# Moving token normalisation and routing weights from VectorE to GpSimd in a transformer layer with attention and experts

## The chip, the cores and the metric

The kernel runs on one core of a Trainium2 chip. The metric is device time in microseconds, from start to end of one execution of the whole program. The core has a matrix engine (TensorE, PE in the profile, with its weight loads PEld), VectorE (DVE), ScalarE (ACT), GpSimd (POOL) and SyncE (SP, which here only issues DMAs). Each engine works through its own instructions in their order, and they wait for one another through semaphores.

## The reference

A batch of 8 sequences of 512 tokens, 128 wide, goes through one pre-normalised layer. All is float32.

```
x = x + attention(layernorm(x))      # 16 heads of 64, relative-position bias, softmax
x = x + experts(layernorm(x))        # 16 experts, each token takes its best 4

logits = -dist2(x, keys) + x @ rw.T + rb
topv, topi = top_k(logits, 4)
w = softmax(topv)
expert(x) = gelu(x @ w1.T + b1) @ w2.T + b2
out = sum(w[k] * expert[topi[k]](x) for k in range(4))
```

## The kernel before

**Attention.** The eight sequences are the batches b = 0 to 7 (`LAST` is 7). A batch has 8 steps i = 0 to 7, one for each pair of heads, and a step has four visits v = 0 to 3, one for each block of 128 queries, with two heads hh in each. So there are 64 steps in a row, all written out. What a step does for its visits is spread over engines: TensorE makes the scores (L1288), VectorE adds the bias and finds the maximum (`scores`, L1020, semaphore `neg_rdy`), ScalarE takes the exponential (L863), VectorE the reciprocal of the sum (L1026, `rinv_rdy`), and GpSimd multiplies the probabilities by it (`normalise_probs`, L795, two instructions of 128x512 a visit, `norm_rdy`). Visits 0 and 1 are then transposed by VectorE (`turn_blocks`, L1036) and by a round trip through DRAM (tile `turned` out to `pt_dram`, back as `pt_d`); visits 2 and 3 by TensorE in the next step (`weights_t`, L1302). TensorE multiplies both by the values (L1314 for the late half, L1325 for the early half, which waits for `pt_d`). In the middle of a step it also projects queries, keys and values for the next step (L1239 to L1241).

**What TensorE waits for in a step.** Visit 3's scores need the first maximum of this step. The second transpose of visit 3 of the step before (L1302, hh = 1) needs the fifth maximum, which VectorE makes as visit 2's first. L1314 needs the seventh maximum, which stands behind VectorE's transposes of visit 0, and these wait for GpSimd's `norm_rdy` of visit 0.

**Routing** of batch b-1 is laid between the steps of batch b by small tables (`ROUTE_DVE`, `ROUTE_POOL`, ...), which give for a step the stages that each engine does there. GpSimd computes the reciprocal deviation (`rstd`, L342) at step 2, visit 2; VectorE normalises the tokens into `copies` (stage 3, L383, in `early_extras`) in step 3; TensorE transposes them (L315) and makes the logits (L320) at the end of step 3; VectorE finds the best four, their slots (L445, L448) and, at the end of step 5, the routing weights (stages 10 to 12, L424, L427, L430). GpSimd scatters the tokens to `xs_dram` with 16 indirect DMAs (L363) from step 5 on; the first of them waits for the slots. In step 6 VectorE normalises the next batch's tokens into `xn` (L383, shown as tile `xt`, which shares its memory), and TensorE transposes them at the step's end (L1233).

**Experts.** After attention, 79 blocks of 256 token rows go through their expert, eight of them in each turn of a loop, some turns written out. TensorE turns a block's rows (L1391), makes the hidden layer (L1403 to L1405) and the second product (L1416); GpSimd scatters the result with two indirect DMAs a block (`block_out`, L830). The last batch's routing is spread over the first blocks by tables named `TAIL_...`. SyncE loads the rows of block 32 only after all token scatters have landed (`rest`). At the end VectorE adds the weighted results to the tokens (`combine`).

Of the kernel before, what the change touches and what calls it, by code (L numbers as in the profile page):

```python
# [29 lines left out]
P = 128  # L30
# [7 lines left out]
def layer_kernel(nc, x, wq, wk, wv, wo, rel_bias, onehot, ident, expert_no, before_tok, region, home_row, pad,  # L38
# [47 lines left out]
    with ExitStack() as ctx:  # L86
# [248 lines left out]
        def route_pool(pool, n, stage_no):  # L335
            if stage_no == "rstd":
# [5 lines left out]
                pool.tensor_tensor(rstd[:, 1], var_eps[:, 1], minus_half[:], ALU.pow).then_inc(rstd2, 1)  # L342
            elif stage_no == "copy":
# [36 lines left out]
        def normalise(dve, n, q, to, ready, done):  # L380
            dve.wait_ge(ready, n + 1)
            for c in range(TC):
                dve.tensor_scalar(to[:, c, :], x_all[:, bass.ds(n * TC + c, 1), :], moments[:, q, c, 0:1],  # L383
                                  rstd[:, q, c:c + 1], ALU.subtract, ALU.mult).then_inc(done, 1)

        def route_dve(dve, n, stage_no):
# [5 lines left out]
            elif stage_no == 3:  # L392
                normalise(dve, n, 1, copies[:, :, 0, 0:D], rstd2, xn2)
# [34 lines left out]
            elif stage_no == 12:  # L428
                dve.wait_ge(ei_rdy, n + 1)
                dve.tensor_tensor(wt[:, bass.ds(n * TC, TC), :], ev[:], einv[:].unsqueeze(2).broadcast_to([P, TC, TOP]),  # L430
                                  ALU.mult).then_inc(wt_rdy, 1)
# [107 lines left out]
        ROUTE_DVE_LATE = {3: (4, 5, 6), 4: (13, 14), 5: (10, 11, 12)}  # L539
# [3 lines left out]
        ROUTE_POOL = {(2, 2): ("rstd",), (3, 2): ("copy",)}  # L543
# [61 lines left out]
        TAIL_DVE = {5: (3,), 7: (4, 5, 6), 8: (7, 8, 9), 9: (10, 11, 13, 14), 10: (12, 15, 16)}  # L605
        TAIL_POOL = {1: ("rstd",), 3: ("copy",)}
        TAIL_POOL.update({8 + q: (2 * q, 2 * q + 1) for q in range(6)})
        TAIL_POOL.update({14 + q: (12 + q,) for q in range(4)})
# [4 lines left out]
        def complete(n):  # L613

            return min(NBLK, max(EARLY + NE, (S * TOP * (n + 1) + NE * (BLK - 1)) // BLK))
        assert max(TAIL_POOL) < PEEL
# [160 lines left out]
        def _(pool):  # L777
# [20 lines left out]
            def step(b, i):  # L798
                for v in range(TC):
# [4 lines left out]
                    if (i, v) == ((4, 1) if b == 0 else (0, 3)) and b < LAST:  # L804
                        rsqrt(b + 1)
                    for n, q in scatters_at(b, i, v):
                        route_pool(pool, n, q)
# [182 lines left out]
        def _(dve):  # L990
# [73 lines left out]
            def early_extras(b, i):  # L1064

                if i == NPR - 2 and b < LAST:
                    normalise(dve, b + 1, 0, xn, rstd_rdy, xn_rdy)
                if i == 3 and exists(b - 1):
                    route_dve(dve, b - 1, 3)

# [38 lines left out]
            def combine(n, k):  # L1109

                dve.wait_ge(ld_y[n % YB][k], 16 * (n // YB + 1))
# [491 lines left out]
```

## Time and profile before

| | |
|---|---|
| time before, median of 3 (lowest to highest) | 1126.33 us (1124.82 to 1127.68) |
| profiled execution: time, span of instructions | 1125.26 us, 1123.4 us |
| busy: TensorE, VectorE, ScalarE, GpSimd | 94%, 77%, 75%, 61% of the span |
| granted TensorE clock, mean | 0.989 of full speed |
| chain that ended last, by engine | PE 75%, DVE 11%, DMA 5%, issue 4%, POOL 4% |

The busy shares say which engine could bound a stage, and the chain says which did. In brackets behind an instruction of a timeline stands how long its engine sat idle before it, and whose end released it. A matmul's end is modelled, and matmuls overlap, so step lengths are better taken from the start of one step's first score matmul to that of the next.

### The profile page before, as it was taken

Reading aid. Unit: us, or ns where it says so; the run is one execution under the profiler, and the core shown is the slowest. Engines: PE = TensorE matmul, PEld = TensorE weight load, DVE = VectorE, ACT = ScalarE, POOL = GpSimd, SP = SyncE. Lnnn points to the kernel's source line nnn. Section 1 sums busy time; section 2 is a strip of 40 time slices with the busy share of each in tenths; the row PEclk is TensorE's granted clock in tenths of the full one; section 3 lists DMA queues with packets and bytes.
Section 4 is the critical chain, followed back from the end, with each engine's and each line's share of the span. In section 5 each row is a group of like instructions: output and inputs, shape, how many; then the busy total and the mean of one; then the engine's idle time right before and its main releaser. Section 6 shows DMA issues by size and latency. Waiting matters only on the chain.

```text
span 1123.4 us, 27427 instructions
## 1 busy us (share of the span) xinstructions
PE 1059.4 (94%) x8477; PEld 863.0 (77%) x8478; DVE 862.0 (77%) x2576; ACT 842.5 (75%) x2050; POOL 684.0 (61%) x882
## 2 busy tenths in 40 slices
PE   8999998999999999999999999999889999999993
PEld 4777776777677777767776776777679999999993
DVE  6788789888888888888988889798726544457775
ACT  5788777877787788778877877787757677766661
POOL 4654545774676477467656755764746777655553
PEclk9999999999999999999999999999989999999997
DMA  7776776665666567567656765687852733224552
GB/s 209 215 213 187 209 218 195 185 186 165 182 188 180 163 192 191 154 180 201 182 154 186 204 167 165 186 258 229 253 168 77 164 87 89 78 77 149 158 173 66
DMA packets 138223, 193.27 MB, mean 172 GB/s; under 512 B 19320, under 2 KB 110976, under 8 KB 138096
## 3 DMA queue, kind: packets, MB, share of 16 engines
q1 hardware_dynamic: 128944, 174.84, 55.6%
q0 software_dynamic: 9152, 16.88, 4.5%
q8 instruction: 62, 1.02, 0.4%
q14 instruction: 65, 0.53, 0.2%
HBM read 103.27 MB, written 90.33 MB: 172 GB/s over the span
## 4 chain that ended last, share of the span: by engine, by line
PE 75%; DVE 11%; DMA 5%; issue 4%; POOL 4%; SPq 1%; ACT 1%; DVEq 0%; POOLq 0%; ACTq 0%
PE bank L1416 12%; PE bank L1288 12%; PE bank L1325 9%; PE bank L1314 9%; PE bank L1302 6%; DVE shared L1020 5%; PE bank L1403 3%; PE bank L1405 3%; PE bank L1404 3%; PE bank L1239 3%; PE bank L1241 3%; PE bank L1240 3%; PE bank L1336 3%; POOL shared L795 3%; DMA pt_d<-pt_dram 2%
## 5 line engine op out<-in xcount | busy, mean ns | idle before, releaser
L795 POOL TENSOR_SCALAR shared<-shared,rinv 128x512 f32<-128x512 f32 x512 | 352.4, 700 | 262.5 <-DVE rinv L1026 260.2
L863 ACT ACTIVATE shared<-shared,nmax 128x512 f32<-128x512 f32 x512 | 367.5, 728 | 85.7 <-DVE nmax L1020 84.5
L1020 DVE CUSTOM_DVE_ANT_0 shared<-bank,shared 128x512 f32<-128x512 f32 x512 | 329.0, 680 | 78.9 <-PE bank L1302 26.9
L830 POOL DMA_INDIRECT y_dram<-yb,home x158 | 160.7, 1017 | 93.4 <-issue 49.0
L1036 DVE STREAM_TRANSPOSE turned<-shared 128x512 f32<-128x512 f32 x256 | 166.3, 687 | 14.1 <-issue 14.1
L363 POOL DMA_INDIRECT xs_dram<-copies,slot x128 | 135.1, 1056 | 61.5 <-issue 47.7
L869 ACT ACTIVATE pt_e<-bank 128x512 f32<-128x512 f32 x256 | 146.6, 595 | 31.1 <-PE bank L1302 30.4
L1302 PE MATMUL bank<-idn,shared 128*128 128x128 f32 x1024 | 139.7, 277 | 18.7 <-DVE nmax L1020 18.6
L1416 PE MATMUL bank<-shared,act_h 128*128 x1264 | 154.1, 275 | 1.2 <-DVE yb L1141 0.7
L1416 PEld LDWEIGHTS bank<-shared,act_h 128*128 128x128 f32 x1264 | 148.0, 192 | 1.8 <-issue 1.8
L1302 PEld LDWEIGHTS bank<-idn,shared 128*128 128x128 f32 x1024 | 112.8, 141 | 45.2 <-issue 29.1
L1314 PE MATMUL bank<-pt_e,v_sb 128*64 128x256 f32 x1024 | 124.6, 385 | 5.2 <-DVE nmax L1020 4.6
L895 ACT ACTIVATE act_h<-bank,shared 128x256 f32<-128x256 f32 x316 | 124.2, 476 | 3.4 <-PE bank L1405 3.2
L1325 PE MATMUL bank<-pt_d,v_sb 128*64 128x256 f32 x1024 | 122.7, 381 | 2.7 <-DMA pt_d<-pt_dram 2.7
L1288 PE MATMUL bank<-k_hi,q_lo 64*128 64x512 f32 x512 | 109.6, 422 | 12.5 <-DVE nmax L1020 9.4
L1314 PEld LDWEIGHTS bank<-pt_e,v_sb 128*64 128x64 f32 x1024 | 69.2, 136 | 52.5 <-issue 23.2
L863 ACT ACTIVATION_READ_ACCUMULATOR shared<-shared,nmax 128x1 f32 x512 | 104.5, 204 | 0.0
L1325 PEld LDWEIGHTS bank<-pt_d,v_sb 128*64 128x64 f32 x1024 | 73.8, 137 | 36.5 <-issue 4.7
L1288 PE MATMUL bank<-k_hi,q_hi 64*128 64x512 f32 x512 | 101.6, 390 | 0.0
L1288 PE MATMUL bank<-k_lo,q_hi 64*128 64x512 f32 x512 | 101.5, 390 | 0.0
L1403 PE MATMUL bank<-xbt_hi,w_lo 128*128 128x256 f32 x316 | 96.2, 305 | 4.1 <-DVE w_lo L1129 4.1
L1141 DVE TENSOR_TENSOR yb<-bank,shared 128x256 f32<-128x256 f32 x79 | 33.5, 425 | 78.7 <-PE bank L1416 78.4
(154 smaller groups left out, 1904.0 us busy)
## 6 DMA issues: line engine op xcount, KB each, us to landing
pt_dram<-turned SPq DMA_DIRECT2D x512, 128.0 KB
pt_d<-pt_dram SPq DMA_DIRECT2D x128, 512.0 KB, 4.4
xb<-xs_dram SPq DMA_DIRECT2D x79, 129.0 KB
shared<-in_experts SPq DMA_DIRECT2D x16, 514.0 KB, 5.3
shared<-y_dram SPq DMA_DIRECT2D x32, 256.0 KB, 5.0
shared<-roll_dram SPq DMA_DIRECT2D x4, 768.0 KB, 8.2
y_dram<-yb,home POOLq DMA_INDIRECT x158
xs_dram<-pad_sb SPq DMA_DIRECT2D x17, 129.0 KB, 2.3
```

The costliest lines, as they stand in the source:

```text
L363: pool.indirect_dma_start(xs_dram, bass.IndirectOffsetOnAxis(ap=slot[:, c * TOP + k:c * TOP + k + 1], axis=0), copies[:, c, k % 2, :], Non ...
L795: pool.tensor_scalar(tile, tile, rinv[:, 2 * v + hh:2 * v + hh + 1], 1.0, ALU.mult, ALU.mult)\
L830: pool.indirect_dma_start(y_dram, bass.IndirectOffsetOnAxis(ap=home[:, j, c:c + 1], axis=0), yb[:, j, c, :], None, bounds_check=last_row, ...
L863: act.activation(prob[:, v, hh, :], prob[:, v, hh, :], ACT.Exp, bias=nmax[:, n:n + 1], scale=-1.0, accum_out=rsum[:, n:n + 1]).then_inc(ex ...
L869: act.activation(pt_e[:, hh, :, (v - 2) * P:(v - 1) * P], weights_bank(b, i, v, hh)[:].rearrange("p (j q) -> p j q", j=TC), ACT.Copy)\
L1020: dve.tensor_tensor_reduce(prob[:, v, hh, :], score_bank(v, hh)[:], strips[:, 2 * i + hh, v * P:v * P + S], -1.0, BIG, ALU.add, ALU.min, n ...
L1036: dve.transpose(turned[:, v, :, :, hh, :].rearrange("p k j r -> p j k r"), prob[:, v, hh, :].rearrange("p (j k c) -> p j k c", k=TC, c=BK) ...
L1288: mm = pe.matmul(score_bank(v, hh)[:], q[rows, i % 2, v * P:(v + 1) * P], k[rows, i % 2, :], start=(m == 0), stop=(m == 2))
L1302: mm = pe.transpose(weights_bank(b, i, v, hh)[:, j * P:(j + 1) * P], prob[:, v, hh, j * P:(j + 1) * P], idn[:])
L1314: pe.matmul(ps_a[DH * hh:DH * hh + DH, 2 * P:4 * P], v_sb[:, i // 2 % 2, j, col:col + DH], pt_e[:, hh, j, :], start=(j == 0), stop=(j == T ...
L1325: mm = pe.matmul(ps_a[DH * hh:DH * hh + DH, 0:2 * P], v_sb[:, i // 2 % 2, j, col:col + DH], pt_d[:, :, :, j, hh, :].rearrange("p v a r -> ...
L1416: mm = pe.matmul(ps_y[:, c * D:(c + 1) * D], act_h[:, q % 2, f, c * P:(c + 1) * P], params[:, bass.ds(w + (W2 + f * D), D)], start=(f == 0 ...
```

## The change

Three pieces of elementwise work go from VectorE's program to GpSimd's: the routing normalisation (to step 2, visit 2, right behind `rstd`), the next batch's normalisation (from step 6 to step 4, visit 3), and the product that makes the routing weights (from the end of step 5 to step 6, visit 1, behind the scatter there). The two instructions before that product stay on VectorE. `combine` waits for the weights through a semaphore, as another engine now makes them. For the last batch, GpSimd issues one token scatter behind each of the blocks 8 to 23, where it issued two behind each of the blocks 8 to 13 and one behind each of the blocks 14 to 17.

```diff
             elif stage_no == "rstd":
...
                 pool.tensor_tensor(rstd[:, 1], var_eps[:, 1], minus_half[:], ALU.pow).then_inc(rstd2, 1)
+                normalise(pool, n, 1, copies[:, :, 0, 0:D], rstd2, xn2)
+            elif stage_no == "weights":
+                pool.wait_ge(ei_rdy, n + 1)
+                pool.tensor_tensor(wt[:, n * TC:(n + 1) * TC, :], ev[:], einv[:].unsqueeze(2).broadcast_to([P, TC, TOP]),
+                                   ALU.mult).then_inc(wt_rdy, 1)
...
-        def normalise(dve, n, q, to, ready, done):
-            dve.wait_ge(ready, n + 1)
+        def normalise(eng, n, q, to, ready, done):
+
+            eng.wait_ge(ready, n + 1)
             for c in range(TC):
-                dve.tensor_scalar(to[:, c, :], x_all[:, bass.ds(n * TC + c, 1), :], moments[:, q, c, 0:1],
+                eng.tensor_scalar(to[:, c, :], x_all[:, n * TC + c, :], moments[:, q, c, 0:1],
                                   rstd[:, q, c:c + 1], ALU.subtract, ALU.mult).then_inc(done, 1)
...
-        ROUTE_DVE_LATE = {3: (4, 5, 6), 4: (13, 14), 5: (10, 11, 12)}
+        ROUTE_DVE_LATE = {3: (4, 5, 6), 4: (13, 14), 5: (10, 11)}
...
-        ROUTE_POOL = {(2, 2): ("rstd",), (3, 2): ("copy",)}
+        ROUTE_POOL = {(2, 2): ("rstd",), (3, 2): ("copy",), (6, 1): ("weights",)}
...
-        TAIL_DVE = {5: (3,), 7: (4, 5, 6), 8: (7, 8, 9), 9: (10, 11, 13, 14), 10: (12, 15, 16)}
+        TAIL_DVE = {7: (4, 5, 6), 8: (7, 8, 9), 9: (10, 11, 13, 14), 10: (15, 16)}
...
-        TAIL_POOL.update({8 + q: (2 * q, 2 * q + 1) for q in range(6)})
-        TAIL_POOL.update({14 + q: (12 + q,) for q in range(4)})
+        TAIL_POOL.update({8 + q: (q,) for q in range(SCATTERS)})
...
+        TAIL_POOL[10] = ("weights",) + TAIL_POOL[10]
...
+                    if (i, v) == (4, 3) and b < LAST:
+                        if exists(b - 1):
+                            pool.wait_ge(l_rdy, b)
+                        else:
+                            pool.wait_ge(xhi_rdy, b + 1)
+                        normalise(pool, b + 1, 0, xn, rstd_rdy, xn_rdy)
...
-            def early_extras(b, i):
-
-                if i == NPR - 2 and b < LAST:
-                    normalise(dve, b + 1, 0, xn, rstd_rdy, xn_rdy)
-                if i == 3 and exists(b - 1):
-                    route_dve(dve, b - 1, 3)
-
...
                 dve.wait_ge(ld_y[n % YB][k], 16 * (n // YB + 1))
+                dve.wait_ge(wt_rdy, n + 1)
...
-                early_extras(b, i)
```

GpSimd's program in batch 1, from step 1's last probabilities to the copies of step 3, before (L342 is the routing's `rstd`, L348 and L349 are the stage "copy"):

```order
L795 TENSOR_SCALAR shared<-shared,rinv 128x512 x14
L342 TENSOR_TENSOR rstd<-var_eps,minus_half 128x4
L795 TENSOR_SCALAR shared<-shared,rinv 128x512 x8
L348 COPY copies<-copies 128x4x128
L349 COPY copies<-home_sb 128x8
L795 TENSOR_SCALAR shared<-shared,rinv 128x512 x12
L363 DMA xs_dram<-copies,slot 69888x129
```

Here two visits' worth of probabilities follow `rstd` directly. The same place now, where L389 is the line in `normalise`, L353, L354 and L368 are the former L348, L349 and L363:

```order
L342 TENSOR_TENSOR rstd<-var_eps,minus_half 128x4
L389 TENSOR_SCALAR copies<-x_all,moments,rstd 128x128 x4
L795 TENSOR_SCALAR shared<-shared,rinv 128x512 x8
L353 COPY copies<-copies 128x4x128
L354 COPY copies<-home_sb 128x8
L795 TENSOR_SCALAR shared<-shared,rinv 128x512 x10
L389 TENSOR_SCALAR xt<-x_all,moments,rstd 128x128 x4
L795 TENSOR_SCALAR shared<-shared,rinv 128x512 x2
L368 DMA xs_dram<-copies,slot 69888x129
```

Four instructions stand in front of visit 3's probabilities of step 2, and four in front of visit 0's of step 5; no other instruction of GpSimd's changed places here.

VectorE's program in batch 1, from the slots of step 5 to the second maximum of step 6's visit 0, and on to its visit 2, before (the ISA rows are the maximum, L1020, and the read of its result):

```order
L1036 STREAM_TRANSPOSE turned<-shared 128x4x4x32 x2
L1026 RECIPROCAL rinv<-rsum 128x2
L424 TENSOR_REDUCE esum<-ev 128x4
L427 RECIPROCAL einv<-esum 128x4
L430 TENSOR_TENSOR wt<-ev,einv 128x16
L1026 RECIPROCAL rinv<-rsum 128x2
L1020 ISA shared,nmax<-bank,shared 128x512
...
L1026 RECIPROCAL rinv<-rsum 128x2
L383 TENSOR_SCALAR xt<-x_all,moments,rstd 128x128 x4
L1020 ISA shared,nmax<-bank,shared 128x512
```

Step 6's first maximum stands behind the product, and visit 2's behind the normalisation. Now (L1042, L1032, L1026 are the former L1036, L1026, L1020):

```order
L1042 STREAM_TRANSPOSE turned<-shared 128x4x4x32 x2
L1032 RECIPROCAL rinv<-rsum 128x2
L428 TENSOR_REDUCE esum<-ev 128x4
L431 RECIPROCAL einv<-esum 128x4
L1032 RECIPROCAL rinv<-rsum 128x2
L1026 ISA shared,nmax<-bank,shared 128x512
...
L1032 RECIPROCAL rinv<-rsum 128x2
L1026 ISA shared,nmax<-bank,shared 128x512
```

The product `wt` is gone from before step 6's maxima and the four normalisations from the middle of them; in step 3 the four L383 into `copies` are gone from the same place.

## Rows read from the trace of the kernel before

**Rows 1.** Who waited for whom: us in total, times, longest; TensorE's waits for VectorE.

```profile
PE bank L1302 <- DVE nmax L1020: 18.6, 15, 2.1
PE bank L1288 <- DVE nmax L1020: 9.4, 7, 1.7
```

**Rows 2.** Stretch, its length, busy time by engine: batch 5's step 2.

```profile
537.73:549.25 11.52, 11.52 (x94) 8.78 (x92) 9.80 (x34) 9.84 (x24) 8.50 (x11) 1.00 0.77 208
```

**Rows 3.** The same view, sums of six steps: step 3, then step 6, batches 1-6.

```profile
sum 88.71, PE 80.34 PEld 60.73 DVE 78.57 ACT 63.30 POOL 51.04; mean PE 13.39 PEld 10.12 DVE 13.09 ACT 10.55 POOL 8.51
sum 90.50, PE 75.27 PEld 55.08 DVE 86.35 ACT 63.37 POOL 58.00; mean PE 12.54 PEld 9.18 DVE 14.39 ACT 10.56 POOL 9.67
```

**Rows 4.** Timeline of TensorE in batch 5's steps 3 and 6: start, us.

```profile
554.03 0.60 PE L1302 MATMUL bank<-idn,shared 128*128 128x128 f32 x4
556.03 0.63 PE L1302 MATMUL bank<-idn,shared 128*128 128x128 f32 x4 [1.40 <-DVE nmax L1020]
561.17 1.06 PE L320 MATMUL bank<-rk,xt 128*128 128x16 f32 x8
591.38 0.50 PE L1288 MATMUL bank<-k_hi,q_lo 64*128 64x512 f32 x2 [1.40 <-DVE nmax L1020]
595.85 0.63 PE L1302 MATMUL bank<-idn,shared 128*128 128x128 f32 x4 [1.16 <-DVE nmax L1020]
598.60 0.60 PE L1233 MATMUL bank<-idn,xt 128*128 128x128 f32 x4
```

**Rows 5.** Timeline of VectorE in the same two steps: the three pieces that move.

```profile
552.87 2.40 DVE L383 TENSOR_SCALAR copies<-x_all,moments,rstd 128x128 f32<-128x128 f32 x4
589.11 1.55 DVE L430 TENSOR_TENSOR wt<-ev,einv 128x16 f32<-128x16 f32 x1
593.16 1.94 DVE L383 TENSOR_SCALAR xt<-x_all,moments,rstd 128x128 f32<-128x128 f32 x4
```

**Rows 6.** GpSimd by group: mean ns of one stands behind the busy time.

```profile
L795 POOL TENSOR_SCALAR shared<-shared,rinv 128x512 f32<-128x512 f32 x512 | 352.4, 700 | 262.5 <-DVE rinv L1026 260.2
L830 POOL DMA_INDIRECT y_dram<-yb,home x158 | 160.7, 1017 | 93.4 <-issue 49.0 <-DVE yb L1141 36.4 <-DVE home L1139 7.9
L342 POOL TENSOR_TENSOR rstd<-var_eps,minus_half 128x4 f32<-128x4 f32 x8 | 8.4, 1049 | 1.2 <-issue 1.2
L348 POOL COPY copies<-copies 128x512 f32<-128x512 f32 x8 | 4.9, 616 | 0.0
L349 POOL COPY copies<-home_sb 128x8 f32<-128x8 f32 x8 | 1.5, 193 | 0.0
```

**Rows 7.** Timeline of GpSimd, batch 5's steps 3 to 5.

```profile
552.25 2.69 POOL L795 TENSOR_SCALAR shared<-shared,rinv 128x512 f32<-128x512 f32 x4
576.52 2.99 POOL L795 TENSOR_SCALAR shared<-shared,rinv 128x512 f32<-128x512 f32 x4 [3.52 <-DVE rinv L1026]
585.48 1.11 POOL L363 DMA_INDIRECT xs_dram<-copies,slot  x1 [4.12 <-issue]
```

**Rows 8.** Timeline, batch 5's step 5: VectorE's transposes of visit 0, TensorE's L1314.

```profile
581.57 1.30 DVE L1036 STREAM_TRANSPOSE turned<-shared 128x512 f32<-128x512 f32 x2
584.04 1.95 PE L1314 MATMUL bank<-pt_e,v_sb 128*64 128x256 f32 x16
```

**Rows 9.** Timeline, batch 5's step 6: reads of the DRAM round trip, and their use.

```profile
590.63 2.38 SPq L675 DMA_DIRECT2D pt_d<-pt_dram  x2
600.91 1.90 PE L1325 MATMUL bank<-pt_d,v_sb 128*64 128x256 f32 x16
```

**Rows 10.** The page, DMA issues: KB each, median us from issue to landing.

```profile
pt_d<-pt_dram SPq DMA_DIRECT2D x128, 512.0 KB, 4.4
```

**Rows 11.** Timeline of GpSimd, batch 7's step 3.

```profile
753.88 1.04 POOL L342 TENSOR_TENSOR rstd<-var_eps,minus_half 128x4 f32<-128x4 f32 x1 [1.18 <-issue]
```

**Rows 12.** Timeline among the experts: GpSimd's last token scatter, TensorE's turn of block 32.

```profile
915.11 0.96 POOL L363 DMA_INDIRECT xs_dram<-copies,slot  x1 [0.30 <-issue]
939.12 0.38 PE L1391 MATMUL bank<-idn,xb 128*128 128x128 f32 x2
```

More of the change, by code:

```diff
@@ L391, in route_dve @@
                 moments_of(dve, n, 1, stage_no, st2, mv2, ve2)
-            elif stage_no == 3:
-                normalise(dve, n, 1, copies[:, :, 0, 0:D], rstd2, xn2)
             elif stage_no == 4:
@@ L427, in route_dve @@
                 dve.reciprocal(einv[:], esum[:]).then_inc(ei_rdy, 1)
[L428 to L431, printed above, removed]
             elif stage_no == 13:
```

## Prediction

> **What bounds the kernel now.** TensorE is busy for nearly all of the span, so I look for the time in which it is not, and for who ends it. The list of waits names two large entries, both for VectorE's maxima: 18.6 us in front of L1302 and 9.4 us in front of L1288, 28.0 us together [rows 1]. The lengths of the steps say where they lie. A step in which nothing is added takes 11.52 us, all of it TensorE's [rows 2]. Over batches 1 to 6, step 3 takes 88.71 / 6 = 14.79 us and step 6 takes 90.50 / 6 = 15.08 us [rows 3], and VectorE is busy for 13.1 and 14.4 us of these. The timeline of TensorE shows one wait in step 3, 1.40 us before the second half of visit 3's transposes, and two in step 6, 1.40 us before visit 3's scores and 1.16 us before the same transposes [rows 4]. All three end with a maximum. In front of those maxima VectorE does just the three pieces that the change moves: 2.40 us of normalisation in step 3, the product of 1.55 us ahead of step 6, and 1.94 us of normalisation in it [rows 5]. So each lies on the path that sets the end, but only as far as TensorE waits.
>
> **What can be had.** Step 6 needs, beside the 11.52 us, the four token transposes; they take 0.53 us, from 598.60 to the next work (four L1302 of the same size are 0.60 long [rows 4]). Its floor is 12.05 us, and 15.08 - 12.05 = 3.03 us can go, of which 2.56 us are the two waits and the rest is TensorE's slow start after each. The two removals are 1.55 and 1.94 us, 3.49 us together, more than the 3.03 us, and no VectorE work replaces them. Six batches give 18.2 us. Batch 0 has only the normalisation, and I give it what that costs in batch 5, some 1.1 us. In batch 7 only the product is removed, and the step has expert loads beside it; I give nothing for it (at most 1.4 us, its wait's size elsewhere).
>
> Step 3 needs 11.52 us, the transposes of the copies (0.53 us as above) and the logits (1.06 us [rows 4]), 13.1 us, with some 0.1 us between them. So 14.79 - 13.2 = 1.6 us can go, but here the work comes back on GpSimd's queue in front of what TensorE needs.
>
> **What one instruction costs on GpSimd.** No row shows a 128x128 normalisation there. Below it is bounded by the copy of 8 elements a partition, 0.19 us, above by the same kind of instruction on 512 elements, 0.70 us, and further off by L342, which takes 1.05 us for 4 elements [rows 6]. Copies say how the cost grows: (616 - 193) / 504 = 0.84 ns per element. The same start-up of 0.19 us and 0.98 ns per element for L795 make 0.19 + 128 x 0.98 = 0.31 us. The subtraction and product are two operations as L795's are, so I take its line and not L342's power. Four one behind another are 1.2 us, and about 0.15 us is added for waiting on `rstd` of its own engine, 1.35 us. The product of 16 elements is near 0.2 us and stands at step 6, visit 1, where nobody waits for it.
>
> The Trainium skill (GPSIMD Engine Reference, Engine selection) speaks against the move: elementwise work belongs on VectorE, as GpSimd takes about twice as long where there are two inputs. With one input tensor it calls the two engines about equal. VectorE's normalisations in step 6 are 1.94 / 4 = 0.49 us each; equal would make the sum some 1106 us, twice as long would end near rival 4. No run here shows either on GpSimd yet.
>
> **Step 3 with GpSimd's four.** They stand between `rstd`, which ends at 552.25, and step 2's last probabilities, 2.69 us for two pairs there [rows 7], so 1.35 us for a pair. TensorE's L1302 halves would without waiting start at 554.03 and 554.56, and they need the two halves of this pair. Their second is ready at 552.25 + 1.35 + 1.35 + 0.05 = 555.0 us. The wait is 0.45 us, and with a restart of 0.15 us and some rounding 0.65 us of the 1.6 us stay. VectorE's transposes of visit 0 wait behind the next pair, until 555.6 and 556.3; the seventh maximum then comes at about 557.5, and TensorE asks for it at about 558.3. Gain: 0.95 us in six batches, 5.7 us. In batch 7, `rstd` itself waits for the scatters before it and ends at 754.92 [rows 11], 1.2 us later in the step than in batch 5, so the wait is 0.45 + 1.2 = 1.65 us, where it is now the longest of its kind, 2.1 us [rows 1]: 0.5 us.
>
> **Step 4 and 5.** The next batch's four stand behind step 4's last pair, which ends at 579.51 [rows 7], and in front of step 5's visit 0. That pair would be done at 580.86 + 1.36 = 582.2, its first half at 581.5; VectorE wants the first at 581.57 and the second 0.65 us later [rows 8]. It fits with nothing left over. TensorE's L1314 at 584.04 leaves another 0.6 us, so the stall here is zero up to about 2.0 us for the four and grows one to one beyond. After this GpSimd idles 4.12 us before the first scatter, which waits for slots [rows 7], and the lateness ends there. Nothing else of its queue is late: with the product gone, VectorE's first maximum comes at 589.8 and TensorE asks at 590.0.
>
> **The round trip through DRAM** is the next limit in step 6. Its second read is issued near 592.7 and lands some 4.4 us later, near 597.2 [rows 9, 10]. TensorE takes it at 600.91, and with 3.03 us gone at 597.9. The read does not start earlier, since GpSimd's slots set it. So 0.7 us are left and I charge nothing.
>
> **Tail.** Matrix work bounds it, and the VectorE work taken out there lies beside it. The token scatters now end behind block 23, not 17. At 916.07 GpSimd is through with them [rows 12] and with the results of 18 blocks; it now has 12 result scatters more ahead of its last token scatter, each 1.02 us [rows 6] and 0.3 us of issue, so that one starts no later than 931.7. With 4 us allowed for it to land (the reads of [rows 10] take 4.4) and 2.2 us to load a block (half of what four times the bytes take [rows 10]), block 32's rows are there by 938, and TensorE turns them at 939.12 [rows 12]. I charge nothing; a microsecond or two more would show one to one.
>
> **Sum.** 18.2 + 1.1 + 5.7 + 0.5 = 25.5 us off the profiled 1125.26 us is 1099.8. That execution is 1.1 us below the median of 1126.33, against which the forecast is 1100.8; I say 1101.
>
> **Rivals.**
> 1. *GpSimd's instructions cost by the piece*, 0.70 us as on 512 elements [rows 6]. Four and the wait are 2.95 us. Step 3 waits 2.05 + 0.2 us where 1.6 us were to go: 0.65 us worse. Step 5 stalls 1.1 us. A batch gains 3.03 - 0.65 - 1.1 = 1.3 us; six give 8, batch 0 nothing, batch 7 waits 3.25 us where it now waits 2.1, 1 us worse: 1119 us. For it: the start-up of this kind of instruction is unseen. Against: copies scale with their elements. 7 in 100.
> 2. *The round trip takes part back.* If the read lands 1 to 1.5 us later (or the write before it does), TensorE waits that much in six batches: 6 to 9 us back, 1107 to 1110. For it: only 0.7 us are left. 12 in 100.
> 3. *No wait on GpSimd at all*: its four take 0.8 us or less (0.2 us each, near the small copies). Then step 3 gives its whole 1.6 us: 1096 to 1097. 15 in 100.
> 4. *The other side: GpSimd becomes the bound.* If an instruction costs what L342 does, 1.05 us, four are 4.35 us. Step 3 then waits 3.65 us for 1.6 us removed, step 5 2.5 us: 2.05 + 2.5 - 3.03 = 1.5 us worse a batch, 9 us in six; batch 0 adds 2.5 - 1.1 = 1.4 and batch 7 2.5, 13 us in all: 1139 us. It decides from about 0.9 us per instruction. Against: L342 is a power. 3 in 100.
> 5. *Nothing moves*, since another engine ends the same waits, ScalarE for one: against it, it idles in both steps (10.55 us busy of 14.8 [rows 3]). 2 in 100.
>
> The forecast has the other 61. The range takes rivals 2 and 3 and most of what lies between: 1095 to 1110. A measurement here tells 0.3%, 3.4 us, from no change: faster 0.93, same 0.04, slower 0.03.
>
> **What would show it.** In the changed profile, step 6 near 12.1 us and step 3 near 13.8; L389 near 0.3 us on GpSimd; no wait before L1302 for a maximum, but some 0.5 us before its second half in step 3, behind GpSimd's probabilities; VectorE idle before its transposes of visit 0 in step 3. The forecast is wrong if L389 takes over 0.5 us, or if L1325 waits for `pt_d` in step 6.

## The result, and the profile after

The change makes the kernel slower: 1131.89 us (median of 13 runs, 1128.18 to 1136.33) against 1126.33 us (13 runs, 1124.07 to 1130.25). The ratio is 1.0048, with a 95% interval of 1.0031 to 1.0064. The profiled execution took 1130.02 us with a span of 1128.2 us, 4.8 us more than the span of before, and its mean granted TensorE clock is 0.984 where it was 0.989.

The page's busy times, and the list of waits, TensorE's alone (us in total, times, longest):

```profile
PE 1061.5 (94%) x8477; PEld 870.4 (77%) x8478; DVE 822.8 (73%) x2508; ACT 841.2 (75%) x2050; POOL 733.8 (65%) x950
```

```profile
PE bank L1301 <- POOL shared L795: 14.7, 7, 2.6
PE bank L1313 <- DVE nmax L1026: 14.0, 14, 1.7
PE bank L1324 <- DMA pt_d<-pt_dram: 6.8, 8, 2.6
...
PE bank L1287 <- DVE nmax L1026: 1.7, 6, 0.5
...
PE bank L1301 <- DVE nmax L1026: 0.6, 1, 0.6
```

L1301 and L1287 are the former L1302 and L1288. Their waits for VectorE, 28.0 us in [rows 1], are gone but for 2.3 us. In their place stand 14.7 us in which the same transposes wait for GpSimd's probabilities, and 14.0 us in front of L1313 (the former L1314). The first seven are the step 3 of each batch with routing; of the 14.0 us, 7.9 (six times 1.31 to 1.33) stand in step 5 of batches 1 to 6.

Now the sums of batches 1 to 6 (the view of [rows 3]) for step 3, step 5 and step 6. The fourth line is step 5 of before:

```profile
sum 97.54, PE 85.45 PEld 64.94 DVE 66.37 ACT 64.23 POOL 69.25; mean PE 14.24 PEld 10.82 DVE 11.06 ACT 10.71 POOL 11.54
sum 77.38, PE 69.46 PEld 56.08 DVE 54.78 ACT 59.68 POOL 54.60; mean PE 11.58 PEld 9.35 DVE 9.13 ACT 9.95 POOL 9.10
sum 77.05, PE 74.43 PEld 55.73 DVE 67.27 ACT 62.01 POOL 58.60; mean PE 12.41 PEld 9.29 DVE 11.21 ACT 10.33 POOL 9.77
```

```profile
sum 69.04, PE 69.04 PEld 53.25 DVE 55.80 ACT 59.72 POOL 38.74; mean PE 11.51 PEld 8.88 DVE 9.30 ACT 9.95 POOL 6.46
```

Step 6 gives 90.50 - 77.05 = 13.5 us back, as meant. Step 3 takes 97.54 - 88.71 = 8.8 us more and step 5 77.38 - 69.04 = 8.3 us more. Batch 0's step 6 is 1.2 us shorter and its step 5 0.8 us longer. What is left of the 4.8 us, some 1.5 us, is mostly made of two parts that no term names: the first score matmul of the program starts 2.4 us earlier (14.62 us where it was 17.05), and batch 0's step 1 takes 3.5 us more, with a wait of 2.61 us for `pt_d` (0.69 us before) and two falls of the granted clock to 0.50, 3.41 us each, where there was one before. What makes that wait longer isn't shown.

What one moved instruction costs, by its line in `normalise` (ns min/median/max), and the product on its new line:

```profile
L389 POOL TENSOR_SCALAR copies<-x_all,moments,rstd x32: 777/782/1065, 151.8 to 851.6; 128x128 f32<-128x128 f32 x32
L389 DVE TENSOR_SCALAR xt<-x_all,moments,rstd x4: 341/344/418, 7.4 to 8.2; 128x128 f32<-128x128 f32 x4
```

```profile
L346 POOL TENSOR_TENSOR wt<-ev,einv x8: 220/224/237, 200.2 to 883.5; 128x16 f32<-128x16 f32 x8
```

A normalisation takes 0.78 us on GpSimd, where the forecast had 0.31. The timeline of batch 5, first GpSimd's around step 3's start, then TensorE's in the same step:

```profile
554.51 1.04 POOL L342 TENSOR_TENSOR rstd<-var_eps,minus_half 128x4 f32<-128x4 f32 x1
555.67 3.12 POOL L389 TENSOR_SCALAR copies<-x_all,moments,rstd 128x128 f32<-128x128 f32 x4
558.78 2.68 POOL L795 TENSOR_SCALAR shared<-shared,rinv 128x512 f32<-128x512 f32 x4
```

```profile
552.57 0.50 PE L1287 MATMUL bank<-k_hi,q_lo 64*128 64x512 f32 x2
...
556.46 1.06 PE L1335 MATMUL bank<-wo_sb,ctxt 128*128 128x128 f32 x8
559.51 1.60 PE L1301 MATMUL bank<-idn,shared 128*128 128x128 f32 x8 [2.00 <-POOL shared L795]
...
569.61 0.50 PE L1287 MATMUL bank<-k_hi,q_lo 64*128 64x512 f32 x2
```

The four end at 558.78; the first of the pair behind them takes 0.67 us, and at about 559.5 TensorE can go on, after 2.00 us. The same in step 5, GpSimd, VectorE and TensorE:

```profile
585.07 3.12 POOL L389 TENSOR_SCALAR xt<-x_all,moments,rstd 128x128 f32<-128x128 f32 x4
588.17 1.36 POOL L795 TENSOR_SCALAR shared<-shared,rinv 128x512 f32<-128x512 f32 x2
```

```profile
588.95 1.33 DVE L1042 STREAM_TRANSPOSE turned<-shared 128x512 f32<-128x512 f32 x2 [1.70 <-issue]
```

```profile
591.01 1.30 PE L1313 MATMUL bank<-pt_e,v_sb 128*64 128x256 f32 x10 [1.32 <-DVE nmax L1026]
```

The profile names no engine for VectorE's wait ("issue"), but the times fit: the first probabilities of GpSimd's pair are done at 588.17 + 0.68 = 588.85, and the transposes start at 588.95. So GpSimd's lateness goes through these transposes, which idle 1.70 us, to the seventh maximum behind them and so to TensorE.

Step 3 has a second loss. Its stretches in batch 5, cut at the wait and at the changes of the clock (length, busy time of PE, PEld, DVE, ACT, POOL, granted clock, DMA share, GB/s):

```profile
552.57:557.40 4.83, 4.83 (x42) 3.97 (x40) 3.70 (x13) 3.30 (x8) 4.11 (x6) 1.00 0.72 187
557.40:559.50 2.10, 0.11 (x1) 0.00 (x0) 0.70 (x4) 1.30 (x5) 2.10 (x4) 1.00 0.73 236
559.50:560.40 0.90, 0.88 (x6) 0.64 (x7) 0.00 (x0) 0.19 (x1) 0.90 (x2) 1.00 0.43 173
560.40:563.80 3.40, 3.40 (x14) 3.11 (x13) 2.59 (x7) 2.37 (x6) 1.82 (x4) 0.50 0.21 53
563.80:569.61 5.81, 5.81 (x47) 3.78 (x45) 4.10 (x20) 3.69 (x9) 2.65 (x5) 1.00 0.48 122
```

After the wait TensorE works at full clock for 0.9 us, and then the granted clock is 0.50, that is 1.2 GHz where it was 2.4, for 3.40 us. It falls so in three of the seven steps 3 with routing in this execution. Of batches 1 to 6, the three without a fall take 15.44 to 15.50 us, the three with one 16.80, 17.26 and 17.04: 4.6 us more together. Some 0.3 us of that is batch 4's own, whose step 3 takes 15.83 us in a_busy, where the clock holds; 4.3 us are left for the clock.

### The profile page after: what moved, and what is told of

It is laid out like the page before. It is cut to its first block and busy times, and to the rows that moved or that the text cites. A ratio compares the mean times of both kernels' runs of the same rounds, so it can differ in the third digit from the quotient of the medians.

```text
span 1128.2 us, 27442 instructions
## 1 busy us (share of the span) xinstructions
PE 1061.5 (94%) x8477; PEld 870.4 (77%) x8478; DVE 822.8 (73%) x2508; ACT 841.2 (75%) x2050; POOL 733.8 (65%) x950
## 5 line engine op out<-in xcount | busy, mean ns | idle before, releaser
L795 POOL TENSOR_SCALAR shared<-shared,rinv 128x512 f32<-128x512 f32 x512 | 350.3, 695 | 229.9 <-DVE rinv L1032 227.0
L1026 DVE CUSTOM_DVE_ANT_0 shared<-bank,shared 128x512 f32<-128x512 f32 x512 | 329.6, 681 | 86.7 <-issue 36.5
L836 POOL DMA_INDIRECT y_dram<-yb,home x158 | 163.8, 1037 | 87.0 <-issue 47.8
L1042 DVE STREAM_TRANSPOSE turned<-shared 128x512 f32<-128x512 f32 x256 | 166.7, 689 | 49.3 <-issue 48.8
L368 POOL DMA_INDIRECT xs_dram<-copies,slot x128 | 134.7, 1053 | 56.9 <-issue 44.0
L1301 PE MATMUL bank<-idn,shared 128*128 128x128 f32 x1024 | 139.5, 278 | 15.3 <-POOL shared L795 14.7
L1301 PEld LDWEIGHTS bank<-idn,shared 128*128 128x128 f32 x1024 | 113.1, 141 | 41.3 <-POOL shared L795 25.7
L1313 PE MATMUL bank<-pt_e,v_sb 128*64 128x256 f32 x1024 | 124.6, 385 | 14.6 <-DVE nmax L1026 14.0
L1324 PE MATMUL bank<-pt_d,v_sb 128*64 128x256 f32 x1024 | 124.7, 385 | 6.8 <-DMA pt_d<-pt_dram 6.8
L1313 PEld LDWEIGHTS bank<-pt_e,v_sb 128*64 128x64 f32 x1024 | 70.9, 136 | 60.7 <-issue 33.0
L1287 PE MATMUL bank<-k_hi,q_lo 64*128 64x512 f32 x512 | 109.5, 422 | 4.7 <-DVE k_lo L1004 2.4
L1324 PEld LDWEIGHTS bank<-pt_d,v_sb 128*64 128x64 f32 x1024 | 76.7, 138 | 40.5 <-issue 12.6
L1287 PE MATMUL bank<-k_lo,q_hi 64*128 64x512 f32 x512 | 101.8, 391 | 0.0
L1287 PE MATMUL bank<-k_hi,q_hi 64*128 64x512 f32 x512 | 101.5, 390 | 0.0
```

Source lines behind the costliest of these rows:

```text
L368: pool.indirect_dma_start(xs_dram, bass.IndirectOffsetOnAxis(ap=slot[:, c * TOP + k:c * TOP + k + 1], axis=0), copies[:, c, k % 2, :], Non ...
L795: pool.tensor_scalar(tile, tile, rinv[:, 2 * v + hh:2 * v + hh + 1], 1.0, ALU.mult, ALU.mult)\
L836: pool.indirect_dma_start(y_dram, bass.IndirectOffsetOnAxis(ap=home[:, j, c:c + 1], axis=0), yb[:, j, c, :], None, bounds_check=last_row, ...
L1026: dve.tensor_tensor_reduce(prob[:, v, hh, :], score_bank(v, hh)[:], strips[:, 2 * i + hh, v * P:v * P + S], -1.0, BIG, ALU.add, ALU.min, n ...
L1042: dve.transpose(turned[:, v, :, :, hh, :].rearrange("p k j r -> p j k r"), prob[:, v, hh, :].rearrange("p (j k c) -> p j k c", k=TC, c=BK) ...
L1287: mm = pe.matmul(score_bank(v, hh)[:], q[rows, i % 2, v * P:(v + 1) * P], k[rows, i % 2, :], start=(m == 0), stop=(m == 2))
```

## The experiments

The first four kernels ran on a chip on which the kernel before took 1163.43 us (11 runs; in the three parts traced there, the time from the first expert block to the end is 34 to 40 us longer than in the kernel before, and attention steps that a part doesn't touch are alike), the later ones where it took 1125.47 (17 runs) and 1125.20 (24 runs). Each ratio is to the kernel before on the same chip.

### m1_forms: what GpSimd's forms cost by themselves

A kernel of its own. It leaves out the whole computation and copies the input to the output; then GpSimd alone runs eight instructions of each form, with nothing beside it, and after it VectorE and then ScalarE do the normalisation.

```
pool.tensor_scalar(out, src(n), mean or 0.25 or none, rstd or 1.5 or 1.0, subtract or mult, mult)
```

> This kernel only copies the input to the output and leaves the whole layer out; beside that, GpSimd alone runs tensor_scalar in twelve forms, eight instructions each, one engine at a time. In the changed kernel one L389 (128 elements, subtraction and product, both operands read from a tile) took 0.78 us, where one L795 (512 elements, two products, one operand read from a tile and one constant) took 0.70. Theory A: the second operand read from a tile is dear: the form with one tile operand and a constant takes 0.3 us at 128 elements (0.19 + 128 x 0.98 ns), whatever the operations, and the form with two 0.78 us. Theory B: the subtraction is dear: every form with it takes 0.78 us, also with constants, and two products 0.3 us also with two tile operands. Theory C: a tensor_scalar costs some 0.7 us by the piece: all forms take 0.6 to 0.8 us at 16, 128, 256 and 512 elements. Theory D: GpSimd is held up in the kernel by VectorE, and all forms take 0.3 us at 128 elements here, where it is alone.

The groups by line. In the output's name s is a subtraction, m a product, p an operand from a tile and i a constant (sm_pp is the change's own form, mm_pi that of L795); m_p is a single product, s_tt a subtraction of two tensors, and the last line is sm_pp on VectorE, run after GpSimd was done:

```profile
L59 POOL TENSOR_SCALAR sm_pp<-x_all,mean,rstd 128x512 f32<-128x512 f32 x8 | 16.5, 2072 | 0.0
L66 POOL TENSOR_SCALAR sm_pp<-x_all,mean,rstd 128x256 f32<-128x256 f32 x8 | 9.6, 1218 | 0.0
L67 POOL TENSOR_TENSOR s_tt<-x_all,mean 128x512 f32<-128x512 f32 x8 | 8.0, 1038 | 0.0
L58 POOL TENSOR_SCALAR sm_pp<-x_all,mean,rstd 128x128 f32<-128x128 f32 x8 | 6.2, 791 | 0.0
...
L61 POOL TENSOR_SCALAR sm_pi<-x_all,mean 128x128 f32<-128x128 f32 x8 | 5.6, 715 | 0.0
L57 POOL TENSOR_SCALAR mm_pi<-x_all,rstd 128x512 f32<-128x512 f32 x8 | 5.4, 692 | 0.0
L63 POOL TENSOR_SCALAR sm_ii<-x_all 128x128 f32<-128x128 f32 x8 | 4.9, 642 | 0.0
L64 POOL TENSOR_SCALAR m_p<-x_all,rstd 128x128 f32<-128x128 f32 x8 | 4.7, 602 | 0.0
L60 POOL TENSOR_SCALAR mm_pp<-x_all,mean,rstd 128x128 f32<-128x128 f32 x8 | 3.4, 447 | 0.0
L65 POOL TENSOR_SCALAR sm_pp<-x_all,mean,rstd 128x16 f32<-128x16 f32 x8 | 3.3, 427 | 0.0
L56 POOL TENSOR_SCALAR mm_pi<-x_all,rstd 128x128 f32<-128x128 f32 x8 | 2.8, 371 | 18.6 <-DMA out<-x_all 18.6
...
L74 DVE TENSOR_SCALAR dve<-x_all,mean,rstd 128x128 f32<-128x128 f32 x8 | 2.1, 342 | 95.1 <-POOL s_tt L67 95.1
```

The pair of operations decides. Two products cost (692 - 371) / 384 = 0.84 ns an element; subtract and multiply cost (2072 - 427) / 496 = 3.3 ns. With constants alone the subtracting form still takes 642 ns against 371 (one tile operand), so it is not the operands: each further tile operand adds about 0.075 us (371 to 447, 642 to 715 to 791). A lone product, 602 ns, is slow as well, so "subtraction is slow" is too narrow; of the forms tried here only two products were quick. And 791 ns alone against 782 in the kernel leaves nothing to contention.

### p_weights, p_routing, p_next: one part of the change each

Each is the kernel before with one piece moved as the change moves it (the tables of the last batch's routing go with it and are left out here).

```diff
 p_weights:
...
-        ROUTE_DVE_LATE = {3: (4, 5, 6), 4: (13, 14), 5: (10, 11, 12)}
+        ROUTE_DVE_LATE = {3: (4, 5, 6), 4: (13, 14), 5: (10, 11)}
...
-        ROUTE_POOL = {(2, 2): ("rstd",), (3, 2): ("copy",)}
+        ROUTE_POOL = {(2, 2): ("rstd",), (3, 2): ("copy",), (6, 1): ("weights",)}
...
 p_routing:
                 pool.tensor_tensor(rstd[:, 1], var_eps[:, 1], minus_half[:], ALU.pow).then_inc(rstd2, 1)
+                normalise(pool, n, 1, copies[:, :, 0, 0:D], rstd2, xn2)
...
-                if i == 3 and exists(b - 1):
-                    route_dve(dve, b - 1, 3)
 p_next:
+                    if (i, v) == (4, 3) and b < LAST:
...
+                        normalise(pool, b + 1, 0, xn, rstd_rdy, xn_rdy)
...
-                if i == NPR - 2 and b < LAST:
-                    normalise(dve, b + 1, 0, xn, rstd_rdy, xn_rdy)
```

> The kernel before with only the routing weights' product moved to GpSimd. Theory 1 (the price of L389 on GpSimd explains the loss, the rest of the prediction holds): this part has no L389, so it shows the gain alone: step 6's first wait of 1.40 us and its restart go in batches 1 to 6, step 6 near 13.5 in place of 15.1 us, 9 to 10 us faster, 1117. Rival (VectorE's time was not what mattered in step 6, or other waits take its place): within 3 us of before.

> The kernel before with only the routing normalisation moved to GpSimd. Theory 1: its four instructions take 3.1 us in front of step 2's last probabilities; step 3 takes 15.5 in place of 14.8 us, 0.7 us in six batches and 0.4 in batch 7, about 4.6 us slower, and more where the granted clock falls below full in step 3 as it did in three of seven in the changed kernel (1.5 us each): 1130 to 1135. Rival (the loss comes from the next batch's normalisation or from the tail): within 2 us of before.

> The kernel before with only the next batch's normalisation moved to GpSimd, to step 4, visit 3. Theory 1: step 5 is 1.4 us longer (12.9 in place of 11.5) in seven batches, and step 6 loses its second wait and restart, 1.3 us or so; the first wait, behind the product, stays. Sum within 2 us of before. Rival (VectorE's 1.9 us in step 6 was all bound, and step 5's stall comes from the product or the slots): 8 us or more faster.

**p_weights** is faster: 1155.39 us, ratio 0.9927 (0.9908 to 0.9945). Step 6 of batches 1 to 6, in the view of sums, is 81.89 us where [rows 3] have 90.50:

```profile
sum 81.89, PE 74.23 PEld 55.13 DVE 77.99 ACT 63.30 POOL 58.68; mean PE 12.37 PEld 9.19 DVE 13.00 ACT 10.55 POOL 9.78
```

That is 1.43 us a batch, 8.6 us in six, and the kernel gains 8.0. This piece alone does nearly what it should (9 to 10 us were expected).

**p_routing** is slower: 1180.51 us, 1.0133 (1.0113 to 1.0153), more than the 1.004 to 1.008 expected of it. Its wait is the changed kernel's 2.00 us, but here all seven steps 3 with routing lose the clock: by the expectation's own prices, 4.6 us for the wait and 1.5 us for each of seven falls make 15.1 us, of the 17.1 measured. Batch 3's step 3, and the sum of six:

```profile
353.66:370.70 17.04, 15.03 (x106) 11.55 (x105) 11.09 (x43) 10.87 (x25) 11.58 (x17) 0.90 0.54 148
...
sum 101.98, PE 90.00 PEld 68.97 DVE 66.49 ACT 65.20 POOL 69.48; mean PE 15.00 PEld 11.50 DVE 11.08 ACT 10.87 POOL 11.58
```

**p_next** is slower too: 1171.69 us, 1.0065 (1.0048 to 1.0082), where no more than 2 us either way was expected. Step 5 takes 12.92 us a batch, as in the changed kernel. Step 6, freed of 1.94 us of VectorE's work, takes 92.33 / 6 = 15.39 us, more than before. The wait behind the normalisation is gone, but the one before visit 3's scores is 1.82 us where it was 1.40 [rows 4], and the mean clock of five of the six steps is 0.89; the first is the one without a fall, though its wait is 2.09 us. It takes 14.30 us where it took 15.36 before, so this piece alone gives back about 1.1 us in step 6 where the clock holds, and loses 1.4 in step 5. The longer wait comes down the queue from GpSimd: in batch 3 VectorE's transposes of step 5's visit 1 idle 1.55 us until the probabilities behind the first scatter are there, and the product and the first maximum stand behind them. TensorE's timeline in batches 1 and 3, then steps 6 of the same two:

```profile
192.07 0.50 PE L1293 MATMUL bank<-k_hi,q_lo 64*128 64x512 f32 x2 [2.09 <-DVE nmax L1026]
...
394.58 0.50 PE L1293 MATMUL bank<-k_hi,q_lo 64*128 64x512 f32 x2 [1.82 <-DVE nmax L1026]
```

```profile
187.65:201.95 14.30, 12.21 (x99) 9.17 (x98) 12.65 (x34) 10.33 (x25) 9.65 (x13) 1.00 0.60 166
...
390.42:406.01 15.59, 13.77 (x98) 10.51 (x96) 12.77 (x34) 10.44 (x25) 9.76 (x14) 0.89 0.53 151
```

The three parts add up to 0.9927 - 1 + 0.0133 + 0.0065 = +1.25%, where the whole is +0.48%: the product and the next batch's normalisation help each other in step 6 (together 13.5 us off in six batches, where the one alone gives 8.6 and the other alone, with its falls, takes 1.8 more), and the clock falls seven times in p_routing's step 3 and five times in p_next's step 6, but three times in the whole change. A part's price read alone was no price in the whole.

### a_cheap: the changed kernel with the cheap form

`normalise` multiplies by `rstd` and by 1.0, as L795 does. It leaves out the subtraction of the mean, so its values aren't those of the reference.

```diff
-                eng.tensor_scalar(to[:, c, :], x_all[:, n * TC + c, :], moments[:, q, c, 0:1],
-                                  rstd[:, q, c:c + 1], ALU.subtract, ALU.mult).then_inc(done, 1)
+                eng.tensor_scalar(to[:, c, :], x_all[:, n * TC + c, :], rstd[:, q, c:c + 1],
+                                  1.0, ALU.mult, ALU.mult).then_inc(done, 1)
```

> The changed kernel with the normalisations in the form whose price is low, one operand from a tile and the constant 1.0, two products: it multiplies by the reciprocal deviation and leaves out the subtraction of the mean (on VectorE for the first batch too). Theory 1 (the prediction's path was right, and only the price of one instruction was wrong): at 0.37 us each, four and the wait are 1.6 us in place of 3.25; step 3 waits 0.7 us on GpSimd and takes 14.0, step 5 takes 11.5 and step 6 12.1 to 12.6 us, no fall of the clock in step 3: 2.0 to 2.3% faster than before (ratio 0.977 to 0.981). Rival (GpSimd's queue costs something of its own in those places, or the round trip through DRAM takes the gain back): 1% faster or less.

1103.90 us, ratio 0.9795 (0.9776 to 0.9814). This one number turns the sign. By its line, the instruction takes:

```profile
L389 POOL TENSOR_SCALAR copies<-x_all,rstd x32: 361/371/651, 150.1 to 827.3; 128x128 f32<-128x128 f32 x32
```

Sums for step 3 (13.82 us each) and step 6 (12.59):

```profile
sum 82.94, PE 80.95 PEld 60.82 DVE 66.37 ACT 62.50 POOL 58.82; mean PE 13.49 PEld 10.14 DVE 11.06 ACT 10.42 POOL 9.80
...
sum 75.55, PE 73.58 PEld 55.78 DVE 65.01 ACT 62.01 POOL 55.69; mean PE 12.26 PEld 9.30 DVE 10.83 ACT 10.34 POOL 9.28
```

Step 5 is 11.53 us but for one batch of 13.61. No step 3 of batches 1 to 6 loses the clock; batch 7's does, behind a wait of 2.61 us. The waits of TensorE for `pt_d` are 8.4 us in all in this kernel, 2.7 before: some of them stand in step 6 (1.07 us in batch 5), which keeps 0.5 us above 12.05.

### a_next50: the changed kernel, the next batch's four one visit later

```diff
-                    if (i, v) == (4, 3) and b < LAST:
+                    if (i, v) == (5, 0) and b < LAST:
```

> The changed kernel with the next batch's normalisation one visit later, behind visit 0's probabilities of step 5 and ahead of the scatter there, where GpSimd sat idle for 4.1 us until the slots came. Theory 1: step 5 is 11.5 us again in place of 12.9 in seven batches, 9.6 us less than the changed kernel, and nothing else moves: 0.3 to 0.5% faster than before on a chip where step 3 loses its clock in some batches, same as before where in all. Rival (what step 5 loses is VectorE's or the slots'): time as the changed kernel.

1119.75 us, 0.9955 (0.9935 to 0.9976): faster than before. Behind visit 0 of step 5 the four lie in the 4.12 us in which GpSimd idles [rows 7]. Step 5 is back at 11.52 us a batch, and step 6 is at 73.72 / 6 = 12.29, so 0.55 us of the changed kernel's 12.84 go with the stall before it. Step 3 is as in the changed kernel, 97.43 us, with three falls. The step's sum:

```profile
sum 69.10, PE 69.10 PEld 53.44 DVE 55.83 ACT 59.73 POOL 57.24; mean PE 11.52 PEld 8.91 DVE 9.31 ACT 9.95 POOL 9.54
```

### a_spread and a_spread_tt: the same work where nobody waits, in two forms

Both put `rstd` a visit earlier, two normalisations in its old place and two behind step 3's visit 0, and the next batch's four behind step 5's visit 0. a_spread_tt also writes each pair as a subtraction and a product of two tensors.

```diff
-        ROUTE_POOL = {(2, 2): ("rstd",), (3, 2): ("copy",), (6, 1): ("weights",)}
+        ROUTE_POOL = {(2, 1): ("rstd",), (2, 2): ("first half",), (3, 0): ("second half",), (3, 2): ("copy",), (6, 1): ("weights",)}
...
-                    if (i, v) == (4, 3) and b < LAST:
+                    if (i, v) == (5, 0) and b < LAST:
...
 a_spread_tt, in normalise:
+            eng.tensor_tensor(to[:, cs, :], x_all[:, n * TC + part[0]:n * TC + part[1], :],
+                              moments[:, q, cs, 0:1].broadcast_to(shape), ALU.subtract).then_inc(centred, 1)
...
+            eng.tensor_tensor(to[:, cs, :], to[:, cs, :], rstd[:, q, cs].unsqueeze(2).broadcast_to(shape), ALU.mult).then_inc(done, h)
```

> The changed kernel with the same instructions in other places of GpSimd's queue: the reciprocal deviation one visit earlier (step 2, visit 1), two of the routing's four normalisations at step 2, visit 2 and two behind visit 0's probabilities of step 3, and the next batch's four at step 5, visit 0. Theory 1: in front of step 2's last probabilities stand 1.6 us in place of 4.2 us, near the 1.05 us of before, so step 3 waits 0.5 us or less, takes 13.3 to 13.8 us and keeps its clock; step 5 11.5, step 6 12.1 to 12.6: 2.0 to 2.5% faster than before. Rival (the transposes of visit 0 in step 3 wait for GpSimd instead, and L1313 after them): step 3 at 14.5 or more, 1.5% faster or less.

> As the one before, with each normalisation as two tensor_tensor over whole halves (the mean, then the deviation, repeated along the tokens' elements), 1.04 us for 512 elements in the forms kernel where four tensor_scalar took 3.1. Theory 1: where the places already hide the work, a cheaper form adds little: within 0.3% of the kernel with the same places. Rival (GpSimd's total load bounds it): 0.5% or more faster than that one.

a_spread: 1099.61 us, 0.9766 (0.9751 to 0.9780). The instructions still cost 0.78 us each, and step 3 still takes 79.46 / 6 = 13.24 us, less than with the cheap form in the old place. a_spread_tt: 1097.51 us, 0.9757 (0.9742 to 0.9771), the best kernel here. It is 2.1 us (0.2%) below the other, within the 0.3% expected; the intervals overlap, and five runs of each don't settle whether the cheaper form gives anything here. Step 3's sums, a_spread first:

```profile
sum 79.46, PE 79.26 PEld 60.47 DVE 66.20 ACT 62.02 POOL 61.28; mean PE 13.21 PEld 10.08 DVE 11.03 ACT 10.34 POOL 10.21
```

```profile
sum 78.53, PE 78.53 PEld 60.82 DVE 65.19 ACT 62.03 POOL 55.81; mean PE 13.09 PEld 10.14 DVE 10.86 ACT 10.34 POOL 9.30
```

TensorE is busy for nearly all of step 3, and the clock falls in none of its seven steps with routing, in either kernel.

### after_again and a_busy: is it the wait, or the clock?

after_again is the changed kernel once more, on a_busy's chip. a_busy keeps GpSimd's order and its late end, but gives TensorE six bfloat16 products of ones to do in the wait, into a bank that nobody reads.

```diff
+                if i == 3 and exists(b - 1):
+                    pe.wait_ge(neg_rdy, TILES * n + 4)
+                    for _ in range(6):
+                        pe.matmul(banks[3][:], ones_bf[:], ones_bf[:].unsqueeze(1).broadcast_to([P, TC, P]), start=True, stop=True)
```

> The changed kernel again, as the base for the next one on the same chip. Both theories: 0.3 to 0.9% slower than before, more in the runs in which step 3 loses its clock more often.

> The changed kernel with six matrix products of ones (128x512, bf16, result not used) on TensorE in step 3 of batches 1 to 7, into the bank that visit 3's transposes write next, so that the wait of 2.0 us for GpSimd is filled for about 1.4 us. Theory 2 (the fall of the granted clock after the wait is a part of the loss, 1.5 us each time): no fall in step 3; step 3 takes 15.5 us in every batch, and the time is below the changed kernel's by 1.5 us for each step that lost its clock there, 3 to 10 us in all. Rival (the clock falls for another reason, or the fall costs nothing on the path): the same time as the changed kernel within 0.2%, and step 3 still has slow ones.

after_again: 1131.84 us, 1.0058 (1.0035 to 1.0081), with the clock down in four of seven steps 3. a_busy: 1126.43 us, 1.0014 (0.9996 to 1.0031), with no fall in any of them: 5.4 us less for 42 matmuls more. Its step 3 in batch 5, and the sum:

```profile
549.07:564.57 15.50, 14.79 (x114) 10.65 (x112) 11.00 (x43) 10.55 (x25) 11.52 (x17) 1.00 0.59 156
...
sum 93.29, PE 88.71 PEld 63.87 DVE 66.38 ACT 63.28 POOL 69.05; mean PE 14.79 PEld 10.64 DVE 11.06 ACT 10.55 POOL 11.51
```

15.50 us is what the changed kernel's step takes where the clock holds. So late probabilities cost 15.5 - 14.8 = 0.7 us a batch against before. In sums of six, the changed kernel's 8.8 us in step 3 are 93.29 - 88.71 = 4.6 us of lateness and 97.54 - 93.29 = 4.3 us of the clock.

### p_tail: the last batch's scatters alone

```diff
-        TAIL_POOL.update({8 + q: (2 * q, 2 * q + 1) for q in range(6)})
-        TAIL_POOL.update({14 + q: (12 + q,) for q in range(4)})
+        TAIL_POOL.update({8 + q: (q,) for q in range(SCATTERS)})
```

> The kernel before with only the last batch's token scatters changed to one behind each of the blocks 8 to 23. Theory 1: TensorE bounds that stage and the rows of block 32 come in time; the same as before within 0.3%. Rival (the rows of block 32 come late, or VectorE's results are freed earlier): more than 2 us either way.

1125.63 us, 1.0005 (0.9988 to 1.0022): nothing, as charged.

## Why the prediction was wrong

The forecast was 1099.8 us for the profiled execution, which took 1130.0: 30.2 us off. By its own terms, six batches each unless said:

| term | forecast | measured | off |
|---|---|---|---|
| step 3 | -5.7 | +8.8 | 14.5 |
| step 5 | 0 | +8.3 | 8.3 |
| step 6 | -18.2 | -13.5 | 4.7 |
| batch 0 | -1.1 | -0.5 | 0.6 |
| batch 7, steps 3, 5 and 6 | -0.5 | +0.4 | 0.9 |
| tail | 0 | -0.3 | -0.3 |
| start, batch 0's step 1, all other steps | not named | +1.5 | 1.5 |

**The step that failed is "What one instruction costs on GpSimd".** It took L795's line, start-up and 0.98 ns an element, since "the subtraction and product are two operations as L795's are", and came to 0.31 us. Measured are 0.78. Both parts of that argument were off. L795 multiplies twice, and m1_forms shows that having two operations isn't enough to have its price: two products cost 0.84 ns an element, subtraction and product 3.3. And the start-up was taken from a copy: by the slope of two products, their own is 371 - 128 x 0.84 = 0.26 us, so even the right form would have been 0.37. The section on cost had bounds of 0.19 and 0.70 us from rows, and said itself that 1.05 us for L342 stood further off; the range was then built on the low end. The prediction's own signs of being wrong both came: L389 takes over 0.5 us, and L1325 (now L1324) waits for `pt_d` in step 6.

**Step 3 and step 5 follow from that number by the prediction's own chain.** Rival 1, given 7 in 100, worked it with 0.70 us: step 3 0.65 us worse, step 5 stalled by 1.1 us. Measured with 0.78 us and the clock up are 0.7 and 1.4 us. "Zero up to about 2.0 us for the four" and one to one beyond gives 1.1 us for 3.12, not far from the 1.4 seen. That rival 1's price was near is luck, since its reason, a cost by the piece, is not what the forms show: 16 elements take 0.43 us and 512 take 2.07. a_cheap shows the chain from the other side: with 0.37 us, step 3 is 13.82 us (forecast 13.8), step 5 11.53 but for one batch, and the kernel 1103.9, in the range. So where the work was put was right for an instruction of 0.3 us and wrong for the real one, and a_spread shows that the real one is harmless elsewhere: its 1099.6 us are near the forecast 1101, but by other places, not by the forecast price.

**The granted clock was in no term and in no rival.** It costs 4.3 us in step 3 of batches 1 to 6 in the profiled execution, and a_busy takes it away with nothing else changed for GpSimd. Rival 4 let the sign turn from about 0.9 us an instruction; with 0.78 it turned already. Put 0.78 us into rival 1's working and the change is still some 2 to 4 us faster than before (an estimate by its rules). Two things take that away: the clock, and the 4.7 us that step 6 does not give back. a_busy, at the same 0.78 us and without the falls in step 3, is within 0.3% of before: there the change is worth about nothing.

**Step 6** was right in mechanism: VectorE's three pieces were what TensorE waited for. It takes 12.84 us against the floor of 12.05. Of the 0.79 us left, 0.55 go with step 5's stall, as a_next50 shows. TensorE still waits 0.23 to 0.49 us for the first maximum in each of the six, and waits for `pt_d` of 0.22 to 0.44 us stand in three of the six. That is rival 2's mechanism at a tenth of its price (0.9 us of 6 to 9); in a_busy one such wait is 1.88 us, so 0.7 us was not much room. **Batch 0** gave 1.2 us in step 6 (forecast 1.1) and lost 0.8 in step 5. **The product** and **the tail** were charged right: the product takes 0.22 us (forecast 0.2) and nobody waits for it, and the end is unchanged.

**The page of the Trainium skill** was weighed and set aside. GPSIMD Engine Reference, Engine selection, has elementwise work about twice as slow on GpSimd with two inputs and roughly at line rate with one, which the prediction read as about equal. The instruction has one input tensor, and it took 791 ns alone against 342 on VectorE in the same kernel (m1_forms): 2.3 times. The direction of its rule, that such work stays on VectorE, was the right warning; what it says of one input fits the form with two products, 371 ns, and none of the subtracting forms measured.

## What to carry to other kernels

Take the price of a moved instruction from the same engine and the same operations, and if the trace has none, let the range run to what the chain does at the dearest row: here two GpSimd instructions of one class and one shape differed by 2.1 times, and everything else followed. Then place the work by the queue: with the same eight dear instructions a batch the change cost 0.5% where they stood in front of what another engine waits for, and gave 2.3% where they lay in GpSimd's slack. Where a change makes a wait of TensorE longer, here from 1.4 to 2.0 us, look at the granted clock behind it in the rows, since that can cost as much as the wait did: 4.3 us against 4.6 here.

## What the runs showed of the hardware

- GpSimd's tensor_scalar on 128 partitions in float32: (product, product) 0.37 us for 128 elements and 0.69 us for 512; (subtraction, product) 0.43, 0.79, 1.22 and 2.07 us for 16, 128, 256 and 512; a lone product 0.60 us for 128. A tensor_tensor subtraction of 512 elements takes 1.04 us, half of the subtracting tensor_scalar's 2.07.
- TensorE, busy before and after it, waits about 2 us (2.00 in the changed kernel's batch 5, 1.80 and 2.31 in its batches 2 and 4), works up to 0.9 us at full clock, and then has 0.50 for 3.40 us: three and four times in seven in two executions of the changed kernel, seven in seven in p_routing on another chip, five in six in p_next after 1.81 to 1.82 us. None of the waits of 1.40 us of the kernel before [rows 4] has a fall behind it. The length of the wait alone doesn't decide: no fall follows 2.13 us in batch 7 of the kernel before, 2.65 us in batch 7 of the changed kernel, or 2.09 us in p_next's batch 1. The Trainium skill (TensorE: Matmul & The Clock Gate, Part 1) says that the gate follows how busy the engine has been lately; a_busy agrees, where TensorE works in the wait and no step 3 has a fall. What decides between three and seven of seven wasn't tried and stays open.
- VectorE's product of 16 elements took 1.55 us in the kernel before, against a least of 0.17 us, by its line:

```profile
L430 DVE TENSOR_TENSOR wt<-ev,einv x8: 170/1550/1554, 188.3 to 864.5; 128x16 f32<-128x16 f32 x8
```

On GpSimd it takes 0.22 us. The Trainium skill (SBUF — State Buffer, Who interferes with whom) has VectorE instructions with two inputs in SBUF contend with a GpSimd instruction that reads there. The rows agree: 1.55 us is about a pair of L795, 1.37 us, and 0.17, and in batch 5 the product runs from 589.11 to 590.66 around a pair from 589.26 to 590.63; but no run here tried it apart.

```profile
589.26 1.37 POOL L795 TENSOR_SCALAR shared<-shared,rinv 128x512 f32<-128x512 f32 x2
```
